# An audio tower and its mixture of experts on one core: the front end moved under the weight loads, the shared expert's down products behind the next chunk's first unit, and the order of a round's last slot

## The reference, cut to what matters

```python
def reference(x, ...):                                   # x: 32 recordings of 40000 samples
    h = tok(x)              # 250 frames each: window, |rfft|^2, mel, log(. + 1e-6), dct, @ w_proj + b_proj -> [32, 250, 192]
    h = h + attn(layernorm(h))
    return h + ffn(layernorm(h))

def attn(x):
    h1 = rmsnorm(x) * norm1_w
    q, k, v = h1 @ wq, h1 @ wk, h1 @ wv                  # 8 heads, 64 / 64 / 24 wide
    qw = einsum('bihd,hdn->bihn', q, w_pos)              # relative positions: 32 basis functions of j - i
    bias = (einsum('bihn,ijn->bhij', qw, basis) + u.k + einsum('hn,ijn->hij', v_param.w_pos, basis)) / 8
    a = softmax(q.k / 8 + bias)
    x = (a @ v).reshape(b, l, 192) @ wo + bo + x
    return gelu((rmsnorm(x) * norm2_w) @ w1 + b1) @ w2 + b2 + x

def ffn(hidden):                                         # 8000 tokens, 16 experts
    scores = sigmoid(x @ gate_weight.T)
    topk_score, topk_ids = top_k(scores.T, 1000)         # each expert takes its 1000 best tokens
    xg = x[topk_ids]
    out = (silu(xg @ Wg.T) * (xg @ Wu.T)) @ Wd.T * topk_score
    y = zeros.at[topk_ids].add(out)
    return y + silu(x @ Ws_g.T) * (x @ Ws_u.T) @ Ws_d.T  # the shared expert
```

## Time and profile before

| | us |
|---|---|
| median of 3 runs | 2059.84 (2055.66 to 2062.31) |
| the profiled execution | 2052.84 |
| its span, first to last instruction | 2051.2 |
| PE busy | 1906.4 (93%) |
| DVE busy | 1363.9 (66%) |
| ACT busy | 1070.8 (52%) |
| POOL busy | 712.3 (35%) |
| mean granted TensorE clock | 0.986 |

### The profile page before, as it was taken

One profiled execution on the slowest core, in us unless ns is written; L12 is line 12 of the kernel. 1 busy time (PEld: TensorE's weight loads), 2 busy tenths in 40 slices (PEclk: granted clock), 3 DMA queues, 4 the chain that ended last, 5 costly groups with the idle time before them and its releaser, 6 DMA issues. The chain is left out here.

```text
span 2051.2 us, 46507 instructions
## 1 busy us (share of the span) xinstructions
PE 1906.4 (93%) x13428; PEld 1634.0 (80%) x13428; DVE 1363.9 (66%) x3748; ACT 1070.8 (52%) x2588; POOL 712.3 (35%) x587
## 2 busy tenths in 40 slices
PE   3899999999999999999976889899999999999996
PEld 2688788888888887888865777788988888898886
DVE  2578878878788788788855777555555555555531
ACT  2687887877878878878751222223222222232221
POOL 0022222222222122222220000456667666667763
PEclk9999999999999999999998999999999999999998
DMA  5556666666666666666655333344445555444451
GB/s 157 162 160 182 183 169 179 181 170 181 177 172 192 166 179 184 169 178 181 173 141 144 97 99 105 90 80 80 81 83 94 87 100 104 83 79 82 84 96 19
DMA packets 318048, 272.95 MB, mean 133 GB/s; under 512 B 80732, under 2 KB 305326, under 8 KB 317998
## 3 DMA queue, kind: packets, MB, share of 16 engines
q1 hardware_dynamic: 238878, 235.53, 42.7%
q0 software_dynamic: 70656, 30.65, 10.3%
q10 hardware_dynamic: 8464, 6.15, 1.0%
HBM read 151.25 MB, written 120.54 MB: 133 GB/s over the span
## 5 line engine op out<-in xcount | busy, mean ns | idle before, releaser
L1212 POOL DMA_INDIRECT out<-ff_y,ff_idxs x128 | 261.7, 2045 | 233.5 <-DVE ff_y L1494 177.9
L1267 ACT ACTIVATE ff_sg<-ffp_g 128x500 f32<-128x500 f32 x192 | 113.0, 589 | 365.4 <-PE ffp_g L1604 365.4
L1199 POOL DMA_INDIRECT ff_xg<-xs_d,ff_idxg x128 | 214.4, 1675 | 245.4 <-issue 232.4
L524 ACT ACTIVATE sb_prob<-sb_ssb,sb_mx 125x250 f32<-125x250 f32 x512 | 253.1, 498 | 61.6 <-DVE sb_rinv L614 33.8
L1479 DVE TENSOR_TENSOR ff_wide<-ff_sg,ffp_u 128x500 f32<-128x500 f32 x192 | 129.3, 673 | 199.9 <-PE ffp_u L1604 199.9
L1618 PE MATMUL ffp_d<-ff_wd,ff_wide 128*125 128x192 f32 x1536 | 259.9, 326 | 1.2 <-issue 0.8
L1604 PE MATMUL ffp_g<-ff_xsp,ff_wsp 128*128 128x500 f32 x960 | 251.1, 392 | 1.6 <-DVE ff_xsp L1355 1.6
L1604 PE MATMUL ffp_u<-ff_xsp,ff_wsp 128*128 128x500 f32 x960 | 249.5, 390 | 0.0
L1618 PEld LDWEIGHTS ffp_d<-ff_wd,ff_wide 128*125 128x125 f32 x1536 | 247.8, 188 | 1.8 <-issue 1.2
L822 PE MATMUL ps_qps<-sb_hsp,sb_wsp 128*128 128x250 f32 x1280 | 184.9, 291 | 31.9 <-DVE sb_hsp L728 22.9
L1604 PEld LDWEIGHTS ffp_u<-ff_xsp,ff_wsp 128*128 128x128 f32 x960 | 181.2, 189 | 37.2
(11 more groups left out here) (190 smaller groups left out, 3550.7 us busy)
## 6 DMA issues: line engine op xcount, KB each, us to landing
bias_d<-sb_rsb SPq DMA_DIRECT2D x256, 219.6 KB
sb_bsk<-bias_d SPq DMA_DIRECT2D x256, 218.8 KB
hx_d<-sb_hx SPq DMA_DIRECT2D x32, 336.0 KB
sb_hxl<-hx_d SPq DMA_DIRECT2D x32, 336.0 KB
ff_wd<-WdT SPq DMA_DIRECT2D x16, 576.0 KB, 6.3
xs_d<-sb_xs SPq DMA_DIRECT2D x32, 238.0 KB
bias_d<-sb_rsb SPq DMA_DIRECT2D x256, 25.5 KB
sb_bsk<-bias_d SPq DMA_DIRECT2D x256, 25.4 KB
```

The costliest lines, as they stand in the source:

```text
L524: a.activation(prob[:, s % 2, t], ssb[:, s % 2, t], ACT.Exp, bias=mx[:, s % 2, t:t + 1], scale=-1.0, accum_out=rs[:, t, s:s + 1]).then_inc ...
L1199: g.indirect_dma_start(xg[:, t], None, xs_d[:, :], bass.IndirectOffsetOnAxis(idxg[:, t:t + 1], 0), bounds_check=last).then_inc(gat[t // HT ...
L1212: g.indirect_dma_start(out_d[:, :], bass.IndirectOffsetOnAxis(idxs[:, t:t + 1], 0), y[:, t], None, bounds_check=last, compute_op=ALU.add). ...
```

## The change

Three places are edited.

1. *Start.* The loads are split over three semaphores and two issuing engines. SP issues the frames, `mel`, `ident`, `n1w` (`t_ld`), then the four weight matrices as one array `wall` (3 DMAs in place of 12), the basis and `u` (`w_ld`), then, after the first DFT product, the frames of batch 1 and nine late loads (`l_ld`), and then the zeros. ACT issues `dft` (`f_ld`), `dct`, `w_proj`, `b_proj` (`t_ld`) and `wqT`, `v`, `w_pos` (`w_ld`). The token stage of batch 0 waits for `f_ld` and `t_ld` alone; the splits of the weights and the fold are called from inside it (`weights_high`, `weights_low`, `fold`, `mel_fold`), and the fold writes to `cps` and `otps`. The first `qk` waits for `ini` 8.
2. *Last slot of a round.* ACT's high half of `hsp` goes between the two exps of slot 7, and its third Gelu from slot 5 to slot 6, behind the `rsb` copies. DVE's low half of `hsp` goes ahead of the LayerNorm statistics, and in slot 0 the `ptsb` copy goes ahead of the scores.
3. *Shared expert and seam.* PE does the down products of chunk c - 1 after unit 0 of chunk c, and the tallies move; DVE's `added`, ACT's store and the last `update` follow; the first split of the next chunk's rows is made after unit 0. The list product of list 0 moves to after unit 0 of chunk 14, its store and its load ahead of the residual load of chunk 15, and constants and expert 0's weights are loaded in chunk 3 in place of chunk 1. For expert 0 the four groups of transposed rows have a PSUM tile each.

The diff, cut to its core:

```diff
+            loads = [(wraw[:, 0], w["wall"][0:128])] + [(wraw[64 * i:64 * i + 64, 1], w["wall"][128:D]) for i in range(2)]
+            for i in range(2):
+                for r in range(2):
+                    loads += [(braw[64 * r + 32 * i:64 * r + 32 * i + 32, i, 0:ND], w["basis"])]
+            loads += [(ucol[:], w["u"])]
+            late = [
...
-            sp.wait_ge(z_set, 3)
+            sp.dma_start(mel[0:BINS], w["melT"]).then_inc(t_ld, 16)
+            sp.dma_start(mel[BINS:2 * BINS], w["melT"]).then_inc(t_ld, 16)
+            sp.dma_start(ident[:], w["ident"]).then_inc(t_ld, 16)
+            sp.dma_start(n1w[:], w["n1w"]).then_inc(t_ld, 16)
+            sp.wait_ge(z_set, 2)
             for dst, src in loads:
                 sp.dma_start(dst, src).then_inc(w_ld, 16)
+            sp.wait_ge(t_mm, 1)
+            load_frames(1)
+            for dst, src in late:
+                sp.dma_start(dst, src).then_inc(l_ld, 16)
+            sp.wait_ge(z_set, 7)
...
+            act.dma_start(dft[:], w["dft"]).then_inc(f_ld, 16)
+            for dst, src in ((dct[:], w["dct"]), (wproj[:], w["w_proj"]), (wmel[MELS:MELS + 1], w["b_proj"])):
+                act.dma_start(dst, src).then_inc(t_ld, 16)
+            act.wait_ge(z_set, 1)
+            act.dma_start(wqT[:], w["wqT"].rearrange("(p r) n -> r p n", r=128)).then_inc(w_ld, 16)
+            act.dma_start(vcol[:], w["v"]).then_inc(w_ld, 16)
+            for i in range(2):
+                for r in range(2):
+                    act.dma_start(wpz[64 * i:64 * i + 64, :, r, i], w["w_pos"].rearrange("(p i d) n -> i d p n", i=2, d=DK)[i]).then_inc(w_ld, 16)
             a.preload_act_table_set(EXP_SET)
...
+            def weights_high():
+                act.wait_ge(w_ld, W_LOADS)
+                for k in range(2):
+                    a.activation(wsp[:, 2 * k, 0:ALL_COLS], wraw[:, k], ACT.Copy).then_inc(w_hi, 1)
+                act.wait_ge(fold_mm, 1)
+                for k in range(2):
+                    for i in range(2):
+                        a.activation(pos_cols(slice(0, 128), 2 * k, i), folded(i, k), ACT.Copy).then_inc(w_hi, 1)
...
+                    if bc is not None and s == 6:
+                        act.wait_ge(c_mm, C_USES * bc + 4)
+                        a.activation(gT[:, 2], tps[:, 0:FRAMES], ACT.Gelu, bias=b1[:, 2:3]).then_inc(c_ev, 1)
...
+                    def model_high():
+                        act.wait_ge(t_mm, T_USES * bt + 4)
+                        if bq is not None:
+                            act.wait_ge(q_mm, Q_USES * bq + QK_USE[-1] + 1)
+                        ps = bank2(tps, FRAMES, 128)
+                        for k in range(2):
+                            a.activation(hsp[:, 0, k], ps[:, k], ACT.Copy, scale=n1w[:, k:k + 1]).then_inc(t_hi, 1)
+
+                    if bb_ is None and bt is not None and s == 7:
...
+                            if t == 0 and bt is not None and s == 7:
+                                model_high()
...
+                    if s == 0:
+                        pt_copy(bc, HEADS - 1)
...
-                    if s == 0:
-                        pt_copy(bc, HEADS - 1)
                     if s > 0:
                         pt_copy(bb_, s - 1)
+                    if bt is not None and s == 7:
+                        ps = bank2(tps, FRAMES, 128)
+                        dve.wait_ge(t_hi, 2 * (bt + 1))
+                        for k in range(2):
+                            ins = v.scalar_tensor_tensor(out=hsp[:, 1, k], in0=ps[:, k], scalar=n1w[:, k:k + 1], in1=hsp[:, 0, k].bitcast(F32),
+                                                         op0=ALU.mult, op1=ALU.subtract)
+                        ins.then_inc(t_ev, 1)
...
+                        if opening(bt):
+                            mel_fold()
...
+                        if opening(bt):
+                            fold()
...
+            if isinstance(e, int) and e == 0:
+                return (tp, gps[0], gps[1], ups[0])[j][:, 0:HALF].rearrange("p (t n) -> p t n", n=TP)
+            return tps
...
+                if isinstance(c, int) and c == CHUNKS - 1:
+                    store_list(0)
+                    load_idx(idxg, ig_ld, 0)
...
+                    if m == 0 and (not isinstance(c, int) or c < CHUNKS - 1):
+                        high(c + 1, 1 - par)
+                    if m == 0 and (not isinstance(c, int) or c > 0):
+                        stored(c - 1, 1 - par)
...
+                    if not first:
+                        update(STEPS * c - 1)
                     count(STEPS * c)
-                    gated(c, par, 0)
                     update(STEPS * c)
                     count(STEPS * c + 1)
+                    low(c + 1, 1 - par)
+                    if not first:
+                        added(c - 1, 1 - par)
+                    if first:
+                        gated(c, par, 0)
+                    update(STEPS * c + 1)
+                    if not first:
+                        gated(c, par, 0)
+                    count(STEPS * c + 2)
                     gated(c, par, 1)
-                    update(STEPS * c + 1)
                     gated(c, par, 2)
-                    count(STEPS * c + 2)
-                    low(c + 1, 1 - par)
-                    update(STEPS * c + 2)
-                    added(c, par)
...
+            def down(c):
+                pe.wait_ge(s_h_ev, MS * (c + 1))
+                for i in range(2):
+                    wait(pe, s_y_ev, 2 * (c - 1) + i + 1)
+                    for t in range(2):
+                        for m in range(MS):
+                            ins = m_(dps[i][:, t], s_hT[:, m, (2 * i + t) * TP:(2 * i + t + 1) * TP], s_wd[:, m], start=m == 0, stop=m == MS - 1)
+                    ins.then_inc(s_d_mm, 1)
 
...
+                    first = isinstance(c, int) and c == 0
                     if search and m == 0:
                         tally(STEPS * c)
+                    if not search and m == 0:
+                        route(c, -1)
+                    if m == 0 and not first:
+                        down(c - 1)
+                    if search and m == first:
+                        tally(STEPS * c + 1)
                     if search and m == 2:
-                        tally(STEPS * c + 1)
+                        tally(STEPS * c + 2)
                     if not search:
                         route(c, m)
...
+                if c == SEARCH + 4 and place == -1:
                     list_mm(0)
```

## The result

The changed kernel takes 2042.72 us (median of 4 runs, 2041.32 to 2043.28), the kernel before, on the same chip, 2058.79 us (4 runs, 2055.66 to 2062.31). The ratio is 0.9926, with a 95% interval of [0.9910, 0.9943]: 16 us faster. The forecast was 2012 us, range 1994 to 2028. The sign was right; two thirds of the gain are missing.

The account below looks back on a forecast made before the run. PE was taken as busy 93% of the span, so only its idle time could be gained. Terms 20.5 + 7.5 + 12 + 6 + 1 = 47 us off the 2059.84 median gave 2012.8, stated as 2012 us, range 1994 to 2028.

Parts of the forecast that it names:

- (a): Kernel start: split loads and a later fold bring the first q/k product earlier, 20.5 us gained, ends 12.9 and 25.
- (b): Tower round's last slot: earlier sb_hsp cuts 0.27 us a round, 7.5 us over 28 rounds, ends -3 and 28.
- (c): Shared stage: down products behind the next chunk's first unit remove PE waits, 12 us gained, between 0 and 16.
- (d): Seam to the experts: four PSUM tiles let PE issue the row transposes together, 6 us gained, ends 2 and 6.5.
- The clock's 1 us: Seam and first expert products: with less idle time the granted clock stays up, 1 us gained, from 0 to 2.
- R2: Start gives little, loads or zeros landing late: 12.9 us or less instead of 20.5, 2020 to 2022 us; chance 0.13.
- R3: Shared stage refills its waits behind a busier DVE: 0 to 3 us instead of 12, 2022 us; chance 0.10.
- R5: Nothing to be told: half-clock stretches and the loop give the gains back, 2058 us; chance 0.02.
- R1: Tower round is limited by PE: 28 x 1.0 us gained instead of 7.5, 1992 us; chance 0.12.
- R4: Slower: last slot's late second exp delays DVE's ptsb copy and lengthens every tower round, 2068 us; chance 0.03.

Follow-up runs that it names:

- one_tile: Changed kernel with the four row transposes ahead of the first expert back in one PSUM tile, each waiting for the reads of the one before: 2046.08 us.
- loads_spread: Changed kernel with constants and first expert's weights spread: constants in chunk 1, gate weights in 2, up weights in 3, down weights in 10: 2035.88 us.
- slot_undone: Changed kernel with only the last-slot edits put back to the old order on ACT and DVE: 2026.51 us.
- edge_rinv_first: edge_moved with only the reciprocals of DVE's slot 0 moved ahead of the scores: 2015.43 us.
- start_only: Kernel before with only the front-end part of the change; slot order, shared stage and seam as before: 2033.96 us.
- best: Changed kernel with DVE's pass cut behind slot 4, reciprocals ahead of scores, zeros ahead of late weights, expert weights spread over chunks 1 to 3: 2005.64 us.
- dve_unroll3: Changed kernel with DVE's loop written out three rounds to a pass, no instruction of a round moved: 2072.31 us.
- edge_moved: Changed kernel with DVE's loop cut elsewhere, a pass running from slot 5 of one round to slot 4 of the next, same instruction order: 2025.71 us.
- rinv_xs: Changed kernel with DVE's slot 0 in the order ptsb copy, reciprocals, sb_xs, scores: 2039.22 us.
- copy_back: Changed kernel with only the ptsb copy put back behind scores and reciprocals in DVE's slot 0: 2045.63 us.
- xs_first: Changed kernel with DVE's sb_xs instructions moved ahead of scores and reciprocals in slot 0, right behind the ptsb copy: 2043.05 us.

## Why the prediction was wrong, by its steps

**(a) The start: right.** 20.5 us forecast; 22.8 at the first q/k product, 17.2 left in the changed kernel's trace, 19.6 and 23.3 (trace, medians) alone. The bias rows were the next limit, as said, but at 35.97 us and not about 34. What they cost behind the wait, a stretch at the lower clock, was not in the sum; one_tile and loads_spread, with the same start and tower, show stretches of 3.4 and 6.8 us where the changed kernel's trace has 3.4 and 20.5, so the length differs between executions.

**(b) The round: this step failed.** It said "DVE does the same instructions in another order" and took the time between sb_h and sb_xs as unchanged, so that the 0.36 us of slack became a gain of 0.27 a round, -7.5 us in all. The time is not unchanged: it grew by 0.75 us, 0.43 for the step from pass to pass that the sb_hsp pair had covered, 0.23 for sb_xs with POOL's copy starting inside it. The trace gives +11.8 us, the medians of slot_undone and changed +16.2: an error of 19 to 24 us, most of what is missing. The lower bound of this step, "a loss of 0.1 a round", stands beside a wait on ACT of 0.09 us and nothing else; a move that takes the last instruction of a pass away needed its own. The step's loop, through PE, sb_x, ACT, DVE and sb_xs, was the right one, the wait did move to sb_xs as said, and edge_rinv_first, without the two losses but with the reciprocals moved as well, gains 0.33 a round on before: close to the 0.27. The 0.28 us for sb_rsb did not go (7.9 / 26 = 0.30).

**(c) The shared stage: right but for a move that was not priced.** The search chunk gains 0.91 (1.0 forecast), the route chunks 3 in all. The prediction says nothing of the expert weights' new place on SP; in chunk 3 it costs 7.6 us. Without it the stage's 2.8 would be 10.4, against 12.

**(d) The seam: right.** 5.4 us (6 forecast), 4.9 by one_tile's trace. The clock's 1 us is not there: from the first to the second group of gate products PE took 3.82 us before and takes 3.87 after (1303.46 - 1299.59), with a stretch at the lower clock in both.

The drain of the tower lost 2.7 us that no step had. It took 93.1 us in the changed kernel, 90.4 before and 90.1 in slot_undone, with 28, 24 and 24 us of it at the lower clock; but one_tile has 24 and 92.5, so the clock alone is not it. The loss goes with the slot: the three traces with the old order (before, start_only, slot_undone) have 90.1 to 90.4, the eleven with the new one 90.7 to 93.7. The clock has a part in it: edge_rinv_first has the 90.7, with 24 us at the lower clock, and best, with the same order, 93.0 with 31. What in the new order sets the rest stays open.

The measured 2042.7 us is none of the rivals' numbers; it lies between the 2022 of R2 and R3 and the 2058 of R5. R1 is out (PE was not the round's limit), R2 out by start_only. R3 names the stage that refilled a wait, by another cause. R4 had the sign of the tower right, and its mechanism wrong: the first ptsb copy waits for no exp, as dve_unroll3's short rounds and edge_moved show. R5's clock stretches are real but cost a few us.

## What to carry to other kernels

Before an instruction is moved away from the end of a loop's pass, look at what then stands last: in this loop a long one without waits covered the engine's step to the next pass and short dependent ones did not, and the place where the loop is cut can be chosen apart from the order of the work. Add up an engine's whole stretch between two events of the limiting loop, idle time and neighbours on POOL included, and do not take a reordered sum as unchanged. And of every load that changes its place in a queue ask which small load now stands behind it, and when that one is due.

## What the runs showed of the hardware

- DVE's step from one pass of this loop to the next costs 0.43 us behind short dependent instructions and nothing behind a 0.86 us pair. With a pass three times as long it costs 3.7 us, with six packets of instructions in every pass, where the short one has none.
- sb_xs (2 x 125x192, fp32) takes 0.93 us when POOL's copy of 125x512 starts 0.2 us behind it (changed, edge_moved, rinv_xs), and in all three it ends 0.11 us after that copy. It takes 0.67 to 0.70 when the copy starts 0.3 to 0.4 us ahead of it, though the two overlap by 0.2 to 0.3 us (before, copy_back, edge_rinv_first), and 0.66 with no overlap (xs_first).
- 2.1 MB of weights issued ahead of 0.5 MB of activations made these land 9 us after their issue; 0.58 MB ahead made 8 us of it (1208.30 to 1216.5) and lengthened chunk 10 by 3.9 us, while 0.77 MB ahead in chunks 2 and 3 of the same run made 6 us of it and cost nothing (11.83 and 11.94 us): the bytes ahead do not tell the cost alone.
